# Experts 0 and 1 applied to each block of nodes in turn, router products behind the first layer

## What is computed

```python
feat = jnp.mean(x, axis=0)              # the batch is 1: feat = x
w = jax.nn.softmax(feat @ Wr + br, axis=-1)
h = jnp.einsum('bfd,edh->bfeh', x, W1) + b1
h = jax.nn.relu(_bn(h, g1, be1, m1, v1))
h = jnp.einsum('bfeh,ehk->bfek', h, W2) + b2
h = jax.nn.relu(_bn(h, g2, be2, m2, v2))
y = jnp.einsum('bfeh,ehd->bfed', h, Wo) + bo
return jnp.einsum('bfed,fe->bfd', y, w)
# x = x + this, with x normalized per node (mean 0, variance 1) as its input
```

## Time and profile before

| what | value |
|---|---|
| time, median of 3 | 1248.12 us (1248.11 to 1248.55) |
| the profiled execution | 1251.13 us |
| its span (first to last instruction) | 1249.3 us |
| PE busy over the span | 992.6 us (79%) |
| DVE, ACT, POOL busy | 787.9, 529.7, 408.4 us |
| first expert product, last expert product | 744.66, about 1242 us |

### The profile page before, as it was taken

How to read it: one execution, slowest core, us unless ns; L and a number is a source line. 1 busy time by engine, 2 the same in 40 slices (tenths; PEclk the granted TensorE clock), 3 DMA queues, 4 the chain that set the end, 5 groups by cost and what they waited for, 6 DMA issues and landing times.

```text
span 1249.3 us, 15586 instructions
## 1 busy us (share of the span) xinstructions
PE 992.6 (79%) x5483; PEld 848.0 (68%) x5483; DVE 787.9 (63%) x1363; ACT 529.7 (42%) x1070; POOL 408.4 (33%) x450
## 2 busy tenths in 40 slices
PE   0997258888887787788755446759999999999997
PEld 0776146766776675676644335659789998999986
DVE  6777236877878686877788863354545555454554
ACT  1200034444434443434423124335556667666663
POOL 0036756666666565656664170000000000000000
PEclk9997679999999898889977657689999999999999
DMA  6323434434433443433454100000000000000002
GB/s 196 125 70 108 121 89 115 116 102 113 125 101 113 109 121 94 120 98 106 122 164 132 57 26 1 1 0 1 26 1 26 1 26 1 26 1 1 1 26 78
DMA packets 51375, 89.39 MB, mean 72 GB/s; under 512 B 10454, under 2 KB 34346, under 8 KB 51277
## 3 DMA queue, kind: packets, MB, share of 16 engines
q0 software_dynamic: 18768, 52.88, 15.7%
q1 hardware_dynamic: 32509, 35.27, 9.2%
HBM read 81.42 MB, written 6.68 MB: 71 GB/s over the span
## 4 chain that ended last, share of the span: by engine, by line
PE 58%; DVE 16%; issue 11%; ACT 7%; another core or an unknown queue 6%; DMA 1%; DVEq 1%; SPq 0%; ACTq 0%; POOL 0%; POOLq 0%
PE bank L861 11%; PE bank L862 11%; PE bank L863 11%; PE bank L739 7%; PE bank L788 4%; PE bank L777 3%; PE bank L802 3%; DVE U L1293 2%; DVE G L1185 2%; PE bank L669 2%; PE bank L698 2%; ACT junk L489 2%; ACT TT L503 1%; PE bank L923 1%
## 5 line engine op out<-in xcount | busy, mean ns | idle before, releaser
L416 POOL DMA_INDIRECT G<-projected_rows,src_l x391 | 375.8, 961 | 291.5 <-issue 106.3
L739 PE MATMUL bank<-G,oh 128*128 128x264 f32 x782 | 216.0, 423 | 101.6 <-issue 77.3
L1438 DVE TENSOR_TENSOR hil<-hid,hil 128x1024 fp32r<-128x1024 f32 (+2 forms) x112 | 122.0, 1089 | 232.2 <-ACT hil L610 232.2
L739 PEld LDWEIGHTS bank<-G,oh 128*128 128x128 f32 x782 | 158.3, 208 | 145.5 <-issue 94.4
L602 ACT ACTIVATE hid<-bank,faff 128x512 f32<-128x512 f32 (+2 forms) x224 | 160.3, 723 | 151.1 <-PE bank L863 147.6
L861 PE MATMUL bank<-ew,hil 128*128 128x256 f32 (+1 forms) x400 | 113.3, 283 | 1.5 <-DVE feat_rows L1450 1.5
L862 PE MATMUL bank<-ew,hil 128*128 128x256 f32 (+1 forms) x400 | 113.2, 283 | 0.0
L863 PE MATMUL bank<-ew,hil 128*128 128x256 f32 (+1 forms) x400 | 113.0, 283 | 0.0
L610 ACT CAST hil<-hid 128x1024 fp32r<-128x1024 f32 (+2 forms) x112 | 105.1, 939 | 9.6
L1185 DVE TENSOR_TENSOR G<-G,bank 128x3072 f32<-128x3072 f32 (+1 forms) x33 | 109.1, 3305 | 0.0
L503 ACT ACTIVATE TT<-bank,baff 128x128 f32<-128x128 f32 x150 | 57.8, 457 | 103.7 <-remote 86.3
(11 more groups left out here) (291 smaller groups left out, 1676.9 us busy)
## 6 DMA issues: line engine op xcount, KB each, us to landing
dstb<-targets SPq DMA_DIRECT2D x32, 384.0 KB
G<-projected_rows,src_l POOLq DMA_INDIRECT x391
projected_rows<-sums SPq DMA_DIRECT2D x25, 132.0 KB, 2.6
x_in<-in_x SPq DMA_DIRECT2D x3, 1024.0 KB, 8.2
U<-in_x SPq DMA_DIRECT2D x24, 128.0 KB, 2.4
out<-feat_rows SPq DMA_DIRECT2D x24, 128.0 KB
TT<-in_W SPq DMA_DIRECT2D x8, 256.0 KB
wqkv<-in_W SPq DMA_DIRECT2D x8, 256.0 KB
```

What stands on the lines that cost most here:

```text
L416: g.indirect_dma_start(out=G[slot][:, c, :], out_offset=None, in_=table[:, :], in_offset=bass.IndirectOffsetOnAxis(ap=src_l[:, grp, c:c + ...
L739: ins = T.matmul(b_seg[g % 2][:, 0:ROW], oh[g % 2][:, c, :], G[g % SLOTS][:, c, :], start=(c == 0), stop=(c == ch - 1))
L1438: V.tensor_tensor(hidl[layer][par][:, :, 0:cols], hid[layer][:, :, 0:cols], hidh[layer][par][:, :, 0:cols].bitcast(F32), ALU.subtract).the ...
```

## The change

The steps are taken from a list, `STEPS`. Its first eight are experts 0 and 1 in turn on blocks 0, 1, 2 and 3; then come expert 0 on blocks 4, 5, 6 and expert 1 on blocks 4, 5, 6; from step 14 on the order is the former one. `PREPARE` says in which iteration a block is prepared: two steps ahead of its first use, that is blocks 1 to 6 in iterations 0, 2, 4, 6, 7, 8. `RATE` does so for the router: block 0 ahead of the loop, but behind first(0), blocks 1 to 6 in iterations 1, 3, 5, 7, 8, 9. In an iteration the router's products and the softmax stand behind the first layer of the next step (before: ahead of it). `SPLIT` has the weights of expert e split in iteration 12 for e = 2 (before: at the end of 9), 15 for 3 (before 16), 22 for 4 (before 23), and so on, now in the middle of an iteration. The bias shares of the output (`shares`, `add_shares`) begin at step 14 instead of 7. All changes of order are made alike in the lists of PE, ACT and DVE.

```diff
--- before.py
+++ after.py
@@ -58,6 +58,14 @@
 BLOCKS = 7
 BLOCK_TILES = [NT // BLOCKS + (i < NT % BLOCKS) for i in range(BLOCKS)]
 FIRST_TILE = [sum(BLOCK_TILES[:b]) for b in range(BLOCKS)]
+STEPS = [(e, i) for i in range(4) for e in range(2)] + [(e, i) for e in range(2) for i in range(4, BLOCKS)]
+STEPS += [(e, i) for e in range(2, NX) for i in range(BLOCKS)]
+FIRST_STEP = {i: STEPS.index((0, i)) for i in range(BLOCKS)}
+LAST_STEP = {e: max(n for n, step in enumerate(STEPS) if step[0] == e) for e in range(NX)}
+PREPARE = {FIRST_STEP[i] - 2: i for i in range(1, BLOCKS)}
+RATE = {FIRST_STEP[i] - 1: i for i in range(BLOCKS)}
+SPLIT = {LAST_STEP[e - 2] + 2: e for e in range(2, NX)}
+SHARES0 = 2 * BLOCKS
 PAIRS = [(t, min(2, NT - t)) for t in range(0, NT, 2)]
 MAXB = 512
 
@@ -520,7 +528,7 @@
                 if e < 2:
                     act.wait_ge(s["g_free"], NG - 3)
                 else:
-                    act.wait_ge(s["y_mm"], (e - 1) * BLOCKS)
+                    act.wait_ge(s["y_mm"], LAST_STEP[e - 2] + 1)
                 A.copy(ew[:, e % 2, 0], raw[e % 2][:, :, :, :]).then_inc(s["w_hi"], 1)
 
             exponentials(0)
@@ -591,7 +599,7 @@
 
             def hidden(n, layer):
 
-                b, par, e = n % BLOCKS, n % 2, n // BLOCKS
+                (e, b), par = STEPS[n], n % 2
                 cols = columns(b)
                 mm, done, hi, lo = (s[f"h{layer + 1}_{x}"] for x in ("mm", "r", "hi", "lo"))
                 for m in range(KC):
@@ -615,31 +623,27 @@
             norm2(0)
             for t, n in HALVES[0]:
                 features2(t, n)
-            rstd(1)
-            norm2(1)
+            hidden(0, 0)
             softmax(0)
-            for t, n in HALVES[1]:
-                features2(t, n)
-            hidden(0, 0)
             total = NX * BLOCKS
             for n in range(total):
-                if n + 2 < BLOCKS:
-                    rstd(n + 2)
-                    norm2(n + 2)
-                if n + 1 < BLOCKS:
-                    softmax(n + 1)
+                if n in PREPARE:
+                    rstd(PREPARE[n])
+                    norm2(PREPARE[n])
                 if n + 1 < total:
                     hidden(n + 1, 0)
-                if n + 2 < BLOCKS:
-                    for t, k in HALVES[n + 2]:
+                if n in RATE:
+                    softmax(RATE[n])
+                if n in SPLIT:
+                    split_weights(SPLIT[n])
+                if n in PREPARE:
+                    for t, k in HALVES[PREPARE[n]]:
                         features2(t, k)
                 hidden(n, 1)
-                if n == BLOCKS:
+                if n == SHARES0:
                     act.wait_ge(s["gt_tr"], 1)
                     A.copy(gT[:, 0:P], bank[6][:, 0:P])
                     A.copy(gT[0:NT * NX - P, P:2 * P], bank[6][0:NT * NX - P, P:2 * P]).then_inc(s["gt_ready"], 1)
-                if n % BLOCKS == 2 and 2 <= n // BLOCKS + 1 < NX:
-                    split_weights(n // BLOCKS + 1)
 
 
         @block.tensor
@@ -863,7 +867,7 @@
                 return T.matmul(out_, ll, rh, start=False, stop=(k == KC - 1))
 
             def first(n):
-                b, e = n % BLOCKS, n // BLOCKS
+                e, b = STEPS[n]
                 cols, par = columns(b), e % 2
                 if b == 0:
                     pe.wait_ge(s["w_hi"], e + 1)
@@ -880,7 +884,7 @@
                     ins.then_inc(s["h1_mm"], 1)
 
             def second(n):
-                b, e, par = n % BLOCKS, n // BLOCKS, n % 2
+                (e, b), par = STEPS[n], n % 2
                 cols = columns(b)
                 pe.wait_ge(s["h1_hi"], n + 1)
                 pe.wait_ge(s["h1_lo"], n + 1)
@@ -925,24 +929,22 @@
 
             for t, n in HALVES[0]:
                 turn2(t, n)
+            first(0)
             scores(0)
-            for t, n in HALVES[1]:
-                turn2(t, n)
-            first(0)
             total = NX * BLOCKS
             for n in range(total):
-                if n + 1 < BLOCKS:
-                    scores(n + 1)
                 if n + 1 < total:
                     first(n + 1)
-                if n + 2 < BLOCKS:
-                    for t, k in HALVES[n + 2]:
+                if n in RATE:
+                    scores(RATE[n])
+                if n in PREPARE:
+                    for t, k in HALVES[PREPARE[n]]:
                         turn2(t, k)
                 second(n)
                 if n >= 1:
                     third(n - 1)
-                if BLOCKS <= n < BLOCKS + 8:
-                    shares(n - BLOCKS)
+                if SHARES0 <= n < SHARES0 + 8:
+                    shares(n - SHARES0)
             third(total - 1)
 
 
@@ -1433,14 +1435,14 @@
 
             def rest_of(n, layer):
 
-                cols, par = columns(n % BLOCKS), n % 2
+                cols, par = columns(STEPS[n][1]), n % 2
                 dve.wait_ge(s[f"h{layer + 1}_hi"], n + 1)
                 V.tensor_tensor(hidl[layer][par][:, :, 0:cols], hid[layer][:, :, 0:cols], hidh[layer][par][:, :, 0:cols].bitcast(F32),
                                 ALU.subtract).then_inc(s[f"h{layer + 1}_lo"], 1)
 
             def add_outputs(n):
 
-                b, e = n % BLOCKS, n // BLOCKS
+                e, b = STEPS[n]
                 dve.wait_ge(s["y_mm"], n + 1)
                 need(dve, s["y_add"], n)
                 for j, nodes_, y in outputs_of(b):
@@ -1455,7 +1457,7 @@
                 for n in range(2 * i - 2, min(2 * i, len(PAIRS))):
                     t, tiles = PAIRS[n]
                     dve.wait_ge(s["bo_mm"], n + 1)
-                    dve.wait_ge(s["y_add"], BLOCKS + i)
+                    dve.wait_ge(s["y_add"], SHARES0 + i)
                     m = mixed[:, t:t + tiles]
                     V.tensor_tensor(m, m, bank[6 + n % 2][:, 0:tiles * F].rearrange("p (t c n) -> p t c n", t=tiles, c=KC), ALU.add).then_inc(s["x2b"], 1)
                     dve.wait_ge(s["x2b"], n + 1)
@@ -1464,36 +1466,32 @@
             statistics(0)
             rstd(0)
             split_weights(1)
-            statistics(1)
             for t, n in HALVES[0]:
                 rest_rows(t, n)
-            rstd(1)
+            rest_of(0, 0)
             softmax_in(0)
-            for t, n in HALVES[1]:
-                rest_rows(t, n)
             softmax_out(0)
-            rest_of(0, 0)
             total = NX * BLOCKS
             for n in range(total):
-                if n + 2 < BLOCKS:
-                    statistics(n + 2)
-                    rstd(n + 2)
-                if n + 1 < BLOCKS:
-                    softmax_in(n + 1)
+                if n in PREPARE:
+                    statistics(PREPARE[n])
+                    rstd(PREPARE[n])
                 if n + 1 < total:
                     rest_of(n + 1, 0)
-                if n + 1 < BLOCKS:
-                    softmax_out(n + 1)
-                if n + 2 < BLOCKS:
-                    for t, k in HALVES[n + 2]:
+                if n in RATE:
+                    softmax_in(RATE[n])
+                if n in SPLIT:
+                    split_weights(SPLIT[n])
+                if n in PREPARE:
+                    for t, k in HALVES[PREPARE[n]]:
                         rest_rows(t, k)
+                if n in RATE:
+                    softmax_out(RATE[n])
                 rest_of(n, 1)
                 if n >= 1:
                     add_outputs(n - 1)
-                if BLOCKS < n < BLOCKS + 8:
-                    add_shares(n - BLOCKS)
-                if n % BLOCKS == 2 and 2 <= n // BLOCKS + 1 < NX:
-                    split_weights(n // BLOCKS + 1)
+                if SHARES0 < n < SHARES0 + 8:
+                    add_shares(n - SHARES0)
             add_outputs(total - 1)
```

## The result

The median after the change is 1264.85 us (1258.82 to 1273.15) against 1248.11 before: a ratio of 1.0135, interval 1.0099 to 1.0172, so slower by 1.0 to 1.7%. The forecast was 1259.6, slower, with a range of 1249 to 1267. The profiled execution took 1258.82 with a span of 1257.0.

The account below looks back on a forecast made before the run. Serial preparation chains of 15 to 17 us bound the expert loop, PE's products the rest. Second(8) at 888.0, less 843.59 and 33.5, gave +10.9, with the weight split +11.5: 1248.1 + 11.5 = 1259.6 us, range 1249 to 1267.

Parts of the forecast that it names:

- Direction and cause: Expert loop: slower (chance 0.80), as the serial preparation stands in six iterations instead of five; 1259.6 us against 1248.1.
- The chain: Preparing iterations: serial path from second-layer product over addition, statistics, rows, activations, remainder and transposes to the next; 15.8 us.
- the signs named: Profile after: first(0) near 731.5, second(0) near 754, gaps of 7 to 8 us, PE full from about 888.
- Start: Ahead of the loop: first(0) takes the router's place and starts at 731.5, 13.2 us earlier.
- Iteration 0: First(0) to second(0): softmax meets POOL, statistics of block 1 from 743.2, then 11.0 us to second(0) at 754.2.
- Iterations 1 to 8: Second(0) to second(8): 9.85 or 12.7 us without preparation, 20.2, 18.9 or 19.6 with; second(8) at 888.0.
- After second(8): From second(8) on: same PE-bound work, except expert 2's weight split ending about 0.6 us late, bounds 0 and 1.5.
- Sum: Whole kernel: 888.0 - 843.59 - 33.5 = +10.9 us, with the weight split +11.5, so 1259.6.
- the covered preparation: Rival: spare time of iterations 1, 3, 5 takes in the next block's statistics; 24 us faster, 1236; chance 0.06.
- The clock: Rival: PE fed without gaps keeps the full level in second-layer groups; 15 us at most, so 1244; chance 0.14.
- The longer half level: Rival: larger idle stretches cost one more half-level product group each, 2.5 us six times; 1274; chance 0.10.
- In idle time: The loss counted as PE idle time: 29.7 us in five iterations before, 45 after in six.

Follow-up runs that it names:

- e8: The kernel after the change with block 1's statistics and normalization moved from iteration 0 to under first(0); first(0) to second(0) 18.6 us, ratio to before 1.0065.
- the second profile: The unchanged kernel after the change, run and profiled once more; median 1262.2 us, ratio to before 1.0099.
- e4: The kernel after the change with unread 512-column products fed into PE's gaps ahead of the transposes in preparing iterations; 1254.5 us, ratio to before 1.0053.
- e3: The kernel after the change with statistics and normalization of blocks 2 to 6 one iteration earlier; 1253.7 us, ratio to before 1.0041.
- e7: The kernel before, own order and router ahead, with statistics one iteration early behind the features and transposes on both sides of second(n); 1240.6 us, ratio 0.9947.

## Why the prediction was right, point by point

- **Direction and cause**: right. The chain stood in each iteration with a preparation, and there were six. Of the signs named, the granted clock of 754 to 888 was 0.79 (wrong if above 0.85), the idle time of iterations 2, 4 and 6 was 8.0, 8.3 and 7.4 us (7 to 8), and PE was full from 883.58. That is earlier than 888, and first(0) than 731.5, because the border itself came 5.9 us earlier in this profile.
- **Start**: first(0) came 6.70 us after the border (725.73 - 719.03) against 19.8 before (744.66 - 724.9), 13.1 earlier; forecast 13.2.
- **Iteration 0**: the step that was off. Forecast 22.7 us from first(0) to second(0), measured 24.1 in both profiles. I let POOL's collision hit L1423, as in the earlier trace rows. It hit the remainder in front of it:

```profile
725.73 0.76 PE L865 MATMUL bank<-frh,ew 128*128 128x512 f32 x1 [1.62 <-DVE frl L1416]
...
731.98 5.52 DVE L1440 TENSOR_TENSOR hil<-hid,hil 128x1024 fp32r<-128x1024 f32 x1 [6.40 <-ACT hil L618]
...
734.31 2.10 POOL L445 TENSOR_TENSOR feat_rows<-feat_rows,sums 128x256 f32<-128x256 f32 x3
...
739.12 1.41 DVE L1399 BATCH_NORM_STATS2 stats<-feat_rows 128x6 f32<-128x256 f32 x4
```

L1440 took 5.52 us for 1.23 and was done 1.1 us after POOL was (736.41). The softmax came only behind it, so the statistics, at 739.12, stood 13.4 us after first(0) instead of 11.7. The chain from there was 10.75 (11.0 forecast). e8 shows that the place of block 1's statistics decides 5.5 of these 24.1 us.
- **Iterations 1 to 8**: forecast 133.8 us from second(0) to second(8), measured 133.7. That it agrees to 0.1 us is luck, as single ones are off by up to 1.7 to either side and the second profile has 132.4: 9.4 (9.85), 20.0 (20.2), 12.9 (12.7), 19.9 (20.2), 13.5 (12.7), 17.2 (18.9), 20.4 and 20.4 (19.6 each). In iteration 6 the half level behind the router didn't come (second(5) took 2.86). Behind gaps, second(4), second(6) and second(7) took 5.26 to 5.27 instead of the 4.5 that I had put. Without the second-layer group the chain was 15.6, 15.7, 14.4, 15.1 and 15.1 us in iterations 2, 4, 6, 7, 8 (15.8, 15.8, 14.5, 15.1, 15.1 forecast). The softmax between remainder and features in iterations 7 and 8 was there:

```profile
880.11 0.96 DVE L1440 TENSOR_TENSOR hil<-hid,hil 128x768 fp32r<-128x768 f32 x1 [3.69 <-ACT hil L618]
...
880.99 0.17 DVE L1423 TENSOR_TENSOR gate<-bank,brb 128x24 f32<-128x24 f32 x1
...
882.43 0.69 DVE L1416 TENSOR_TENSOR frl<-bank,frh 128x512 fp32r<-128x512 f32 x1 [0.83 <-ACT frh L592]
```

From 880.11 to 882.43 it is 2.32 for a three-tile remainder of 0.96.
- **After second(8)**: 373.4 us, against 405.7 before less 33.5 for the 16 tiles, so 1.2 more; forecast 0.6 for the split of expert 2's weights. That wait was there, with 0.50 us:

```profile
916.06 1.76 DVE L1364 TENSOR_TENSOR ew<-TT,ew 128x1536 fp32r<-128x1536 f32 x1 [0.58 <-ACT ew L532]
...
917.92 0.47 PE L865 MATMUL bank<-frh,ew 128*128 128x512 f32 x1 [0.50 <-issue]
```

DVE was done at 917.82 and first(14) started at 917.92. Of the rest, 0.4 is third(7), partly at the half level (3.53 us, third(3) before 3.11).
- **Sum**: +11.5 forecast, +13.6 and +11.9 measured from split to end, +12.7 on average. The +13.6 of the first profile divide so: from the border to second(0) 8.8 less (30.8 against 39.7); one chain more, 15.2 (five in 75.9 us from second(0) to second(8), four in 60.7 from second(0) to second(4) before); 6.7 that the second-layer groups lost by the half level beyond what they lost before (eight in 36.0 us against four in 18.4, at 2.75 each when full); 0.7 less, as the rest of the 16 tiles' work took 21.8 us instead of 22.5 (33.5 less four groups of 2.75); 1.2 more at the end. In the second profile the eight groups took 34.8, which is most of what the two differ by. The median's +16.7 is larger by some 4 us, which lie ahead of the border or in the uncertainty (12 to 22); the second comparison gave 1.0099. That part isn't explained, and no run tells it from chance. I had written that a measurement can tell 0.2%; the interval of this one is 0.4% to either side.
- **The rivals**: the covered preparation fell: statistics(2) at 768.50 stood behind the addition, as the list has it. The clock kept its half level; e4 prices the part behind gaps at 9.5 to 11 us in the kernel after. The kernel before lost time by it too, so only the difference, 5 to 7 us by the groups' lengths above, belongs to what the change cost; no run feeds the kernel before, and none tells this share from the chain's by experiment. The longer half level fell with iteration lengths of 20.4 at most. The Trainium skill, page "SBUF — State Buffer", section "Who interferes with whom", has a DVE instruction with two SBUF inputs contend with a GpSimd instruction that reads SBUF. The trace agrees: L1440 too has two, and took 5.52 us for 1.23. I used the rule for the wrong instruction.
- **In idle time**: 45 us forecast, 50.3 measured. 12.5 of them were in iteration 0, where the forecast had 7.5 for an average one: first(0), the router and first(1) took only 4.2, 2.6 and 3.0 us, partly at the full level, and the iteration itself was 1.4 longer, so PE waited the longer.

## What to carry to other kernels

Where each engine has a written list, more work between two preparations covers nothing while the preparation stands in the lists ahead of that work: count the serial chains and what each holds, per engine, before counting idle time. Moving a step out of one chain is only a gain if it doesn't land in front of the next one; e3 lost that way, and e7 in part. The order that lost 1% by itself gave the fastest kernels once the lists were uncoupled (2.4% faster than before), so an order of steps is to be judged together with the place of each step in its list.

## What the runs showed of the hardware

- A DVE subtraction of 128x1024 with two SBUF inputs, 1.23 us alone, took 5.52 us beside POOL's multiplications and additions, across three groups of them (each instruction 0.6 to 0.7 us), and was done 1.1 us after POOL was; in e8, 2.35 us and again 1.1 us. Small DVE instructions of 4 columns got through between POOL's in 0.5 to 0.7 instead of 0.17 us (e8, from 739.75).
- PE's granted level fell to half (1.2 GHz) for a part of the group behind 24 back-to-back products of 8 columns, with no gap before or after, in three of three places of e4 (4.4 us for a group of 2.8) and in two of three of the kernel after (granted clock 1.00 over the router's products from 756.68 to 759.28, 0.61 over the group from 759.28 to 763.70; in iteration 6, 1.00 in both).
